# Rotary attention: head units in pairs, alternating score matmuls, V as the stationary operand, probabilities divided on GpSimd before they are transposed

## What is computed

```
def _layer(x, wqkv, qs, ksc, wo, ...):            # 8 heads of 64, windows of 128
    h = shift_token(x)
    q, k, v = split(h @ wqkv)                      # 512 columns each
    q, k = l2norm(q) * qs, l2norm(k) * ksc
    q, k = rotary_xpos(q, k)                       # t*cos*scale + rotate_half(t)*sin*scale
    # each window of 128 queries sees its own 128 keys and the 128 before them
    sim = where(mask, -max, (8 * q) @ k.T)         # 128 x 256 for each head
    o = softmax(sim) @ v                           # 128 x 64 for each head
    x = x + o @ wo
    ...
```

## Time and profile before

| what | value |
|---|---|
| runs | 4908.69, 4920.05, 4929.43 us; median 4920.05 us |
| the profiled execution, first to last instruction | 4908.8 us; the page gives no other time of it, and the lowest run is 4908.69 us |
| mean granted PE clock | 0.900 of full speed |
| first rotary layer: from its first hT matmul to its last take_out | 2837.3 to 3470.2 us |
| second rotary layer: its 33 take_outs | 3906.5 to 4490.4 us |
| PE busy over the whole span | 4331.1 us, 88% |

### The profile page before, as it was taken

How to read it: one execution, slowest core, us unless ns; L and a number is a source line. 1 busy time by engine, 2 the same in 40 slices (tenths; PEclk the granted TensorE clock), 3 DMA queues, 4 the chain that set the end, 5 groups by cost and what they waited for, 6 DMA issues and landing times. The chain is left out here.

```text
span 4908.8 us, 71554 instructions
## 1 busy us (share of the span) xinstructions
PE 4331.1 (88%) x23249; PEld 2982.9 (61%) x23250; DVE 2249.6 (46%) x5734; ACT 1413.8 (29%) x4622; POOL 1258.3 (26%) x1134
## 2 busy tenths in 40 slices
PE   4999999994996499999998989999687899996875
PEld 3676777762664377777775656676343466764442
DVE  4555555552555334333331156666223466664223
ACT  1333333331111222222222234444111244442111
POOL 2333333333223311111111033343101233432000
PEclk9999999996998578777779989999888999998887
DMA  3000000004001200000001010000100000001003
GB/s 102 2 1 2 1 1 1 2 1 154 30 30 64 89 1 1 1 1 1 1 1 55 17 35 6 9 6 6 55 12 9 28 6 9 6 6 52 12 11 104
DMA packets 102500, 115.02 MB, mean 23 GB/s; under 512 B 11384, under 2 KB 92428, under 8 KB 101516
## 3 DMA queue, kind: packets, MB, share of 16 engines
q1 hardware_dynamic: 97292, 98.38, 6.0%
q0 software_dynamic: 4992, 13.64, 0.8%
HBM read 66.91 MB, written 27.26 MB: 19 GB/s over the span
## 5 line engine op out<-in xcount | busy, mean ns | idle before, releaser
L636 ACT ACTIVATE win_probs<-win_score,win_negmax 128x128 f32<-128x128 f32 (+2 forms) x1170 | 464.1, 405 | 1324.3 <-DVE win_negmax L766 1324.3
L396 POOL TENSOR_TENSOR win_probs<-win_probs,win_rsum 128x512 f32<-128x512 f32 (+1 forms) x420 | 422.7, 1007 | 1465.1 <-DVE win_rsum L781 771.7
L766 DVE TENSOR_REDUCE win_negmax<-win_score 128x2 f32<-128x512 f32 (+2 forms) x422 | 283.0, 671 | 945.5 <-PE win_score L522 479.2
L1498 PE MATMUL ffn_hidden<-ffn_hT,ffn_weights_w 128*128 128x512 f32 x640 | 321.0, 662 | 153.3 <-DVE ffn_inner L1590 151.4
L1779 PE MATMUL rot_lin<-rot_weights_w_qkv,rot_hT 128*128 128x512 f32 x816 | 404.9, 619 | 7.5 <-ACT rot_qk L1875 5.5
L1903 ACT ACTIVATE rot_probs<-rot_probs,rot_negmax 128x256 f32<-128x256 f32 x520 | 260.0, 501 | 366.6 <-DVE rot_negmax L1971 366.6
L1498 PEld LDWEIGHTS ffn_hidden<-ffn_hT,ffn_weights_w 128*128 128x128 f32 x640 | 133.7, 214 | 332.7 <-issue 169.8
L794 DVE COPY win_probsT<-win_turned 128x512 f32<-128x512 f32 (+1 forms) x416 | 276.2, 664 | 93.0 <-PE win_turned L532 92.5
L516 PE MATMUL win_score<-win_KT,win_QT 32*128 32x256 f32 x1036 | 294.4, 403 | 0.0
L1817 PE MATMUL rot_score<-rot_KT,rot_QT 64*128 64x256 f32 x1040 | 292.9, 406 | 0.0
L532 PE MATMUL win_turned<-keep_ident,win_probs 128*128 128x128 f32 x1600 | 287.8, 306 | 0.0
(11 more groups left out here) (271 smaller groups left out, 7912.4 us busy)
## 6 DMA issues: line engine op xcount, KB each, us to landing
weights_w<-in_L_ffn_W SPq DMA_DIRECT2D x16, 512.0 KB
scratch_rows_in<-keep_xn SPq DMA_DIRECT2D x1, 5120.0 KB, 16.5
experts_rows<-scratch_rows_in SPq DMA_DIRECT2D x40, 128.0 KB, 2.0
scratch_rows_out<-experts_y POOLq DMA_DIRECT2D x40, 128.0 KB, 2.0
rot_weights_w_qkv<-in_L_ffn_wqkv SPq DMA_DIRECT2D x3, 1536.0 KB, 6.5
rot_h<-keep_xn SPq DMA_DIRECT2D x36, 128.0 KB
rot_h<-keep_xn SPq DMA_DIRECT2D x36, 127.0 KB
keep_xn<-in_L_attn_x SPq DMA_DIRECT2D x4, 1024.0 KB, 9.4
```

The lines of the kernel that those rows point to most:

```text
L396: pool.tensor_tensor(mine, mine, bcast(rsum[:, u % 4, 0:heads], [P, heads, keys]), ALU.mult)\
L636: last = act.activation(probs[:, u % 4, i * width:(i + 1) * width], score[u % 4][:, i * width:(i + 1) * width], ACT.Exp, bias=negmax[:, u ...
L766: dve.tensor_reduce(negmax[:, u % 4, 0:heads], score[u % 4][:, 0:heads * keys].rearrange("p (h k) -> p h k", h=heads), AX.X, ALU.max, nega ...
L1498: last = pe.matmul(hidden[m % RING][k][:], w1[:, c, a:a + P], hT[:, c, :], start=(c == 0), stop=(c == KC - 1))
```

## The change

Three things change in `rotary_attention`, and the orders of all engines are written anew around them.

- Units go in pairs, v = 2n and 2n+1 for a tile. A pair has four heads in two halves, half 0 in rows 0 to 63 and half 1 in rows 64 to 127 of QT and KT. The score matmuls of a pair alternate between the halves, each half into its own bank. Maxima, exponentials, divisions and turns stay per half; `weigh` is one block per pair.
- In `weigh`, V (128 x 64) is the stationary operand and probsT (128 x 128) moves. The output is already transposed: half 0 goes to partitions 0 to 63 of `po`, half 1 to 64 to 127, alternating. ACT copies `po` to oT (`take_attn`); `attn`, the four `oT` transposes and `normalise` go.
- The division by the sums moves ahead of the turn: DVE takes the reciprocals of each half's two sums (`invert`), POOL multiplies 128 x 512 probabilities with them in place (`divide` on POOL), and only then PE turns them.

Besides: ACT copies the turned bank for half 1 and DVE for half 0; probsT has four slots for two, and its memset on POOL doubles; `times_cos` is one instruction of 1024 columns for two of 512, `times_sin` two of 512 for four of 256. POOL's order interleaves the four divisions with the square, the power and the cosines.

```diff
-    plan = [(("q", 2), ("k", 2)), (("QT", 1), ("KT", 1)), (("v", 2), ("oT", -1)), (("hT", 3), ("out", -1))]
+    per_tile = [("q", 2), ("k", 2), ("QT", 1), ("KT", 1), ("v", 2), ("out", -1), ("hT", 3)]
...
+                def divide(it, v, half):                                    # POOL
+                    pool.wait_ge(inverse_ready[half].sem, inverse_ready[half].at(it, v + 1))
+                    mine = probs[:, unit(v, half), :].rearrange("p (j k) -> p j k", j=2)
+                    pool.tensor_tensor(mine, mine, bcast(rsum[:, unit(v, half), :], [P, 2, 2 * P]), ALU.mult)\
+                        .then_inc(probs_ready[half].sem, 1)
...
                         for n in range(TPG):
-                            square_up(b * GPB + gi, n + 2)
-                            times_cos(b * GPB + gi, gi, n + 2)
+                            divide(it, 2 * n + 1, 0)
+                            square_up(it, n + 2)
+                            divide(it, 2 * n + 1, 1)
+                            invert_norms(it, n + 2)
+                            divide(it, 2 * n + 2, 0)
+                            times_cos(it, gi, n + 2)
+                            divide(it, 2 * n + 2, 1)
...
+                    for j, c in enumerate(chunks_of(v)):                    # scores, PE
+                        for half in range(2):
+                            rows = slice(RD * half, RD * (half + 1))
+                            last = pe.matmul(score[unit(v, half)][:, j * 2 * P:(j + 1) * 2 * P], QT[rows, n % 2, c, :],
+                                             KT[rows, c, first:first + 2 * P], start=True, stop=True)
...
+                def turn(it, v, half):
+                    pe.wait_ge(probs_ready[half].sem, probs_ready[half].at(it, v + 1))
+                    other = probsT_ready[1 - half]
+                    pe.wait_ge(other.sem, other.at(it, v + half))
...
+                    for j, c in enumerate(chunks_of(v)):                    # weigh, PE
                         for kb in range(2):
-                            last = pe.matmul(po[:, a:a + RD], probsT[:, u % 2, (2 * j + kb) * P:(2 * j + kb + 1) * P],
-                                             V[:, n % TPG + kb, a:a + RD], start=(kb == 0), stop=(kb == 1))
+                            for half in range(2):
+                                a = (2 * c + half) * RD
+                                last = pe.matmul(po[RD * half:RD * (half + 1), c * P:(c + 1) * P],
+                                                 V[:, n % TPG + kb, a:a + RD],
+                                                 probsT[:, unit(v, half), (2 * j + kb) * P:(2 * j + kb + 1) * P],
+                                                 start=(kb == 0), stop=(kb == 1))
...
+                    for n in range(TPG):                                    # PE's order
+                        linear_step(g, "q", n + 2)
+                        scores(g, 2 * n + 1)
+                        turn(g, 2 * n, 0)
+                        linear_step(g, "k", n + 2)
+                        turn(g, 2 * n, 1)
+                        weigh(g, 2 * n - 1)
+                        linear_step(g, "QT", n + 1)
+                        linear_step(g, "KT", n + 1)
+                        linear_step(g, "v", n + 2)
+                        scores(g, 2 * n + 2)
+                        turn(g, 2 * n + 1, 0)
+                        linear_step(g, "out", n - 1)
+                        turn(g, 2 * n + 1, 1)
+                        linear_step(g, "hT", n + 3)
+                        weigh(g, 2 * n)
...
+                    for n in range(TPG):                                    # ACT's order
+                        linear_step(g, "q", n + 2)
+                        softmax(g, 2 * n + 1, 0)
+                        linear_step(g, "k", n + 2)
+                        take_turned(g, 2 * n)
+                        softmax(g, 2 * n + 1, 1)
+                        linear_step(g, "QT", n + 1)
+                        linear_step(g, "KT", n + 1)
+                        take_attn(g, n - 1)
+                        linear_step(g, "v", n + 2)
+                        softmax(g, 2 * n + 2, 0)
+                        take_turned(g, 2 * n + 1)
+                        linear_step(g, "hT", n + 3)
+                        softmax(g, 2 * n + 2, 1)
...
+                    for n in range(TPG):                                    # DVE's order
+                        rotate(it, n + 1)
+                        maxima(it, 2 * n + 1, 0)
+                        take_turned(it, 2 * n)
+                        maxima(it, 2 * n + 1, 1)
+                        invert(it, 2 * n + 1, 0)
+                        invert(it, 2 * n + 1, 1)
+                        norms(it, n + 2)
+                        maxima(it, 2 * n + 2, 0)
+                        take_turned(it, 2 * n + 1)
+                        maxima(it, 2 * n + 2, 1)
+                        take_out(it, n - 1, lin[i % 2])
+                        invert(it, 2 * n + 2, 0)
+                        divide(it, n + 2)
+                        invert(it, 2 * n + 2, 1)
+                        times_sin(it, gi, n + 2)
```

More of the change, by code:

```diff
@@ L1784, in linear_work @@
                                                 keep.ident[:])
-                    elif name == "oT":
+                    else:
                         pe.wait_ge(attn_ready.sem, attn_ready.at(it, m + 1))
-                        for c in range(RI // P):
-                            last = pe.transpose(lin[:, c * P:(c + 1) * P], attn[:, c * P:(c + 1) * P], keep.ident[:])
-                    else:
                         for c in range(RI // P):
@@ L1802, in linear_step @@
                     linear_work(it, name, m, lin[i % 2])
-                def scores(it, u):
-                    n, heads = heads_of(u)
-                    bank = score[u % 4]
-                    pe.wait_ge(max_ready.sem, max_ready.at(it, u - 3))
-                    if u == 0:
-                        pe.wait_ge(act_took.sem, prologue.index(("KT", 0)) + 1)
-                    elif u % ST == 0:
-                        i = order.index(("KT", n))
-                        pe.wait_ge(*taken(it, i))
-                    for j in range(2):
-                        c, half = divmod(heads[j], 2)
-                        rows = slice(RD * half, RD * (half + 1))
-                        first = n % TPG * P
-                        last = pe.matmul(bank[:, j * 2 * P:(j + 1) * 2 * P], QT[rows, n % 2, c, :],
-                                         KT[rows, c, first:first + 2 * P], start=True, stop=True)
-                    last.then_inc(scores_ready.sem, 1)
@@ new lines, in turn @@
+                def turn(it, v, half):
+                    pe.wait_ge(probs_ready[half].sem, probs_ready[half].at(it, v + 1))
+                    other = probsT_ready[1 - half]
+                    pe.wait_ge(other.sem, other.at(it, v + half))
+                    for i in range(4):
+                        last = pe.transpose(turned[:, i * P:(i + 1) * P], probs[:, unit(v, half), i * P:(i + 1) * P],
+                                            keep.ident[:])
+                    last.then_inc(turned_ready[half].sem, 1)
@@ L1886, in take @@
                             last = act.activation(KT[:, :, 0:P], by_chunk, ACT.Copy)
-                    else:
-                        last = act.activation(oT[:].rearrange("p c n -> p (c n)"), lin[:], ACT.Copy)
                     last.then_inc(act_took.sem, 1)
                 def linear_step(it, name, m):
-                    if name != "out":
-                        i = order.index((name, m))
-                        act.wait_ge(lin_ready.sem, lin_ready.at(it, i + 1))
-                        take(name, m, lin[i % 2])
@@ new lines, in linear_step, with softmax @@
+                    act.wait_ge(lin_ready.sem, lin_ready.at(it, i + 1))
+                    take(name, m, lin[i % 2])
+                def softmax(it, v, half):
+                    u = unit(v, half)
+                    act.wait_ge(max_ready[half].sem, max_ready[half].at(it, v + 1))
+                    for j in range(2):
+                        of_head = probs[:, u, j * 2 * P:(j + 1) * 2 * P]
+                        last = act.activation(of_head, of_head, ACT.Exp, bias=negmax[:, u, j:j + 1], scale=-1.0,
+                                              accum_out=sums[:, u, j:j + 1])
+                    last.then_inc(exp_done[half].sem, 1)
@@ new lines, in take_turned, with take_attn @@
+                def take_turned(it, v):
+                    act.wait_ge(turned_ready[1].sem, turned_ready[1].at(it, v + 1))
+                    act.wait_ge(pv_done.sem, pv_done.at(it, v - 1))
+                    act.activation(probsT[:, unit(v, 1), :], turned[:], ACT.Copy).then_inc(probsT_ready[1].sem, 1)
+                def take_attn(it, n):
+                    act.wait_ge(pv_done.sem, pv_done.at(it, 2 * n + 2))
```

(17 more changed lines are left out.)

192 lines of the change are left out of this document (84 added, 108 removed).

## The result

The changed kernel takes 4939.34 us in the median of 13 runs (4901.95 to 4946.94), the kernel before 4917.06 on the same chip (13 runs, 4902.45 to 4929.43). The ratio over all of these runs is 1.0035, with a 95% interval of 1.0019 to 1.0052 (the quotient of the two medians is 1.0045): a third to a half of a per cent slower, inside the half per cent that the prediction calls no change. The forecast was 5006, and the time lies inside its range. The profiled executions are 4908.8 us before and 4923.0 after, 14.2 apart. Executions of the changed kernel differ in the clock that they were granted, from 0.892 in the shortest to 0.880 in the longest; the profiled one, whose run took 4924.72, had 0.886 and the median one 0.883, so the figures from the profile show the change a little too mild.

The account below looks back on a forecast made before the run. The prediction took PE to bound the kernel at 18.57 us a tile. An 18.0 us cycle plus 1.9 for clock gave 19.9; 64 x (19.9 - 18.57) + 1 = +86 us took the 4920 median to 5006, range 4775 to 5110.

Parts of the forecast that it names:

- What bounds the kernel: Rotary tiles before the change: PE bound, busy throughout the 18.57 us tile at full clock.
- PE's new work: PE per tile: 14.8 us with the halves overlapping, 18.1 without; a pair's scores and weigh about 1.1 each.
- Rival D: PE's scores and weigh: halves don't overlap, each 0.85 more on the cycle; 4992 to 5140 us, chance 0.14.
- The port between DVE and POOL: Shared SBUF port: two-input DVE instructions and POOL's take turns, closing the cycle at 18.0 us instead of 15.8.
- The two halves of the cycle: End of `rotate` to DVE's `divide` issued at 10.45 us, then on to the end of `rotate` at 18.0.
- the prediction's signs: Signs in the profile: tiles near 20 us, clock 0.7 to 0.9, `divide` above 1.3, sines and `rotate` near 2.
- rival C: DVE and POOL don't get in each other's way; cycle 15.8 us, clock holds, 4745 us, chance 0.22.
- theory A: The forecast itself: port waits set an 18.0 us cycle, lost clock makes it 19.9; 5006 us, chance 0.48.
- PE's idle time: PE in each tile: stands still about 3.0 us before turn (2n,1) and 0.8 before `v`.
- The clock: PE's blocks on the cycle, 7.75 us, run at a mean grant of 0.80: 1.9 us more a tile.
- The edges: Layer starts and ends: longer memset, first division and its reciprocal, less work at the end; together +1 us.
- Rival B: The port costs what was forecast but the clock stays; cycle 18.0 us, 4884 us, chance 0.16.

Follow-up runs that it names:

- experiment 5: Changed kernel with half 1's scores made again from half 0's rows of q and k, its own left out: 4959.16 us, ratio 1.0088.
- experiment 2: Changed kernel with POOL's division of (2n+2,1) made to wait until DVE's `rotate(n+2)` is over: 4826.8 us, ratio 0.9828.
- experiment 3: Changed kernel with POOL's divisions cut to 4 of 256 columns for each head: 4784.17 us, ratio 0.9736.
- experiment 1: Changed kernel with three unused matmuls of 512 columns added on PE between k and turn (2n,1): 4889.64 us, ratio 0.9951.
- experiment 6: Changed kernel with the division of (2n+2,1) behind `rotate` and two unused matmuls of 512 columns before turn (2n,1): 4827.14 us, ratio 0.9815.
- experiment 7: Changed kernel with one unused matmul of 512 columns added on PE between k and turn (2n,1): 4913.06 us, ratio 0.9992.
- experiment 10: Kernel of experiment 9 with ACT's copies of k and the turned bank of (2n,1) ahead of the exponentials of (2n+1,0): 4871.53 us, ratio 0.9914.
- experiment 9, with the late division: Kernel of experiment 9 with POOL's division of (2n+2,1) also moved behind `rotate`: 4882.34 us, ratio 0.9930.
- experiment 9: Changed kernel with DVE's copy of the turned bank of (2n,0) moved between the two sines in three tiles of four: 4949.81 us, ratio 1.0066.
- experiment 4: Changed kernel with each pair's scores run one half after the other instead of alternating: 4924.78 us, ratio 1.0023.
- experiment 8: Changed kernel with POOL's division reading one SBUF tensor, as per-head multiplications by a scalar per partition: 4959.81 us, ratio 1.0081.
- experiment 10, with the late division: Kernel of experiment 10 with POOL's division of (2n+2,1) also moved behind `rotate`: 4927.78 us, ratio 1.0022.

## Why the prediction was wrong, point by point

- **What bounds the kernel, and PE's new work: right.** PE's work in a tile was put at 14.8 us, and 15.0 are measured. The scores' block (1.1 for 1.13) and the weigh's (1.1 for 1.09) were right. Rival D is refuted, and experiment 5 shows what it would have cost for the scores: 0.85 for the block on the cycle, its figure. No run put the weigh's two halves in the same columns.
- **The port between DVE and POOL: right in the sum, wrong in the order.** The prediction let the first sine slip in before the cosines and put the division of (2n+2,1) on `rotate`. In fact the first sine waits for all the cosines (2.82), the second for the division (1.52), and `rotate` has its 1.23. The two halves of the cycle were forecast at 10.45 and 7.55 and are 10.31 and 7.71, so the cycle at full clock, forecast at 18.0, is 18.05; that the order inside came out otherwise and the sum did not is in part luck. Of the prediction's signs, `rotate` near 2 us and `divide` above 1.3 failed (1.23 and 1.20). Its sign for rival C, under 8.1 us from `divide` to the end of `rotate`, separated nothing, since its own walk for theory A has 7.55 there. DVE's reciprocals, whose cost beside POOL it had left open, take 0.15 to 0.17 in all 260 cases. Experiments 2 and 3 show that these waits are on the cycle (rival C is refuted: without the last of them a tile takes 17.2, and with hardly any division 16.55).
- **PE's idle time: right in place and nearly in size.** 3.0 before turn (2n,1) for 2.92; 0.8 before v for 0.25. Those two forecasts add up to 3.8, where its own cycle of 18.0 less 14.8 of work leaves 3.2; the full-clock tiles have 3.0.
- **The clock: the step that failed.** It was the right mechanism, put at 1.9 us a tile, and it is 0.72: (19.50 - 18.05) x 31/62. The prediction took a mean grant of 0.80 over the blocks on the cycle in every tile, from the windows of other stages. That is 0.4 x (7.75 + 1.9) = 3.9 us at half clock a tile. In the profile it is 122.4 us in 62 tiles, 2.0 a tile: the 31 tiles that lose clock have the 3.9 us that were forecast, and pay 1.45 for them instead of 1.9; the other 31 have none. That the loss comes in every tile was taken over from other stages, and that is what failed. The 1.2 us that are too much are 75 us over 64 tiles; 5006 less 75 is 4931, 8 from the measured 4939 (the profile that these figures come from is of an execution 15 us under the median). Experiment 1 measures the term by itself: with PE kept busy the time falls by those 41 us, 0.65 a tile (0.71 by the mean of the tiles, 18.77 to 18.06).
- **The edges: right in the sum.** +1 was forecast, and 14.2 less the 13 of the tiles leaves about 1. Its parts were not measured.
- **Small sums.** Three sets of transposes are 1.6 and not 1.5, and PE's work without any overlap is 18.0 and not 18.1. Neither moves the forecast.

The gain on PE, 3.6 us a tile, went into the chain through `divide`, cosines, sines and `rotate`: 3.0 into PE's waits, and 0.7 more into PE's clock that those waits took away. Rival B, the cycle of 18.0 without a loss of clock, was priced at 4884; experiment 1 is that case as to the clock, 4889.64.

Left open: which idle pattern costs the clock. PE's idle time in a full-clock tile, with the number of tiles of 62 that have half clock, is as follows:

| kernel | PE idle in a full-clock tile, us | its longest wait, us (mean) | tiles with half clock |
|---|---|---|---|
| experiment 1 | 0.5 | 0.3 | 0 |
| experiment 6 | 0.5 | 0.3 | 0 |
| experiment 3 | 1.5 | 1.3 | 0 |
| experiment 2 | 2.2 | 2.0 | 8 |
| experiment 5 | 2.2 | 1.9 | 17 |
| experiment 7 | 2.2 | 1.9 | 27 |
| experiment 10 | 2.3 | 2.2 | 20 |
| experiment 9, with the late division | 2.7 | 2.3 | 18 |
| experiment 9 | 2.9 | 1.6 | 37 |
| changed kernel | 3.0 | 2.8 | 31 |
| experiment 4 | 3.0 | 2.8 | 30 |
| experiment 8 | 3.3 | 2.9 | 38 |
| experiment 10, with the late division | 3.3 | 2.2 | 31 |

The count goes with the sum rather than with the longest wait, but experiments 2 and 7, with like sums and like waits, are far apart. So neither figure is a rule, and each count is of one execution.

## What to carry to other kernels

When a change takes work from the engine that is the bound, walk the other engines' orders through one whole cycle before counting the gain: here 3.6 us off PE became 0.5 at full clock, because DVE and POOL wait for each other. PE's idle time then cost 0.7 us a tile on top of itself, by stretches at the 1.2 GHz level. Size such a loss from the time at half clock that rows of a like pattern show, and keep both ends of the range: a mean grant taken from another stage was off by more than a factor of two. And look first at what stands in the way of the late instruction: one division moved behind `rotate` is worth 2.1 points of the ratio here (1.0035 to 0.9828). Two such moves are not the sum of their gains; walk the pair as well.

## What the runs showed of the hardware that I had not expected

- Matmuls on different row halves overlap without being alternated in the program: 8 fp32 records of 64 x 256 take 1.14 us half after half, and 1.13 alternated, against 1.99 when both halves use the same rows (experiments 4 and 5).
- The waits between DVE and POOL are not symmetric. A two-input DVE instruction waits for a two-input tensor_tensor of POOL (2.82 for 0.68) and not for a one-input tensor_scalar (0.69), while POOL's waits for DVE even with one input (2.71 for 1.82). The Trainium skill, "GPSIMD Engine Reference", section Specifications, says that DVE contends with POOL when it has two SBUF inputs. The trace agrees for the 2.82; that section doesn't say what POOL must be doing, and in experiment 8 that decides whether DVE waits.
- A one-input tensor_scalar of 128 x 256 on POOL takes 0.92 us, not half of the 1.04 that a two-input tensor_tensor of 128 x 512 takes.
- Added matmuls whose results nobody reads made a kernel 0.8% faster (the ratios 1.0035 and 0.9951, experiment 1).
